# Row gathers made during the count fill: GpSimd waits for every second pair to land

## What is computed

```
feat = (h @ W).reshape(N, H, D)
e = leaky_relu(el[src] + er[dst], 0.2)
ex = exp(e - segment_max(e, dst)[dst])
alpha = ex / segment_sum(ex, dst)[dst]
rst = segment_sum(feat[src] * alpha[..., None], dst) + bias
...
h = z @ W
msg = h[row] * norm[:, None]
z = segment_sum(msg, col) + b
```

## Time and profile before

| | us |
|---|---|
| timed runs (3) | 5558.09, 5565.08, 5570.45 |
| median | 5565.08 |
| span of the profiled execution | 6940.0 |
| GpSimd busy / VectorE busy / TensorE busy | 2148.9 / 3284.3 / 4623.5 |
| mean granted TensorE clock | 0.815 |

### The profile page before, as it was taken

One profiled execution on the slowest core, in us unless ns is written; L12 is line 12 of the kernel. 1 busy time (PEld: TensorE's weight loads), 2 busy tenths in 40 slices (PEclk: granted clock), 3 DMA queues, 4 the chain that ended last, 5 costly groups with the idle time before them and its releaser, 6 DMA issues. The chain is left out here.

```text
span 6940.0 us, 113554 instructions
## 1 busy us (share of the span) xinstructions
PE 4623.5 (67%) x23328; PEld 3590.1 (52%) x23329; DVE 3284.3 (47%) x10456; ACT 2960.7 (43%) x7576; POOL 2148.9 (31%) x2057
## 2 busy tenths in 40 slices
PE   2411111366565677777777479799999998369997
PEld 1300000233323555555555479677777776369997
DVE  6511111487666666666666745533334333522222
ACT  0200000266666555555555523256655665623332
POOL 2477777300002555555555222100000000422221
PEclk8655555698767888888888589899999999589999
DMA  4377676322224656665566456547753444556665
GB/s 131 113 212 199 193 202 194 116 89 95 95 93 131 165 164 166 169 168 167 163 167 166 127 162 181 146 145 223 221 177 93 133 134 117 165 155 181 181 181 168
DMA packets 623736, 1084.57 MB, mean 156 GB/s; under 512 B 74390, under 2 KB 502093, under 8 KB 616748
## 3 DMA queue, kind: packets, MB, share of 16 engines
q1 hardware_dynamic: 504252, 733.75, 35.3%
q0 software_dynamic: 112144, 268.88, 15.3%
q10 hardware_dynamic: 7200, 80.28, 2.8%
HBM read 782.21 MB, written 309.57 MB: 157 GB/s over the span
## 5 line engine op out<-in xcount | busy, mean ns | idle before, releaser
L740 POOL DMA_INDIRECT arena<-table,arena x1664 | 1667.0, 1002 | 1909.3 <-DVE arena L877 1481.3
L686 PE MATMUL banks<-arena 128*128 128x392 bf16 x2368 | 654.0, 432 | 1198.9 <-issue 846.0
L1416 PE MATMUL banks<-parts,a_wide 128*128 128x512 f32 x4900 | 1179.9, 399 | 17.9 <-ACT a_wide L1439 17.9
L940 PE MATMUL banks<-arena 128*128 128x261 f32 x3328 | 1157.6, 487 | 0.0
L686 PEld LDWEIGHTS banks<-arena 128*128 128x128 bf16 x2368 | 342.1, 151 | 1510.6 <-issue 1470.8
L1416 PEld LDWEIGHTS banks<-parts,a_wide 128*128 128x128 f32 x4900 | 918.3, 189 | 262.9 <-ACT a_wide L1439 47.2
L1439 ACT CAST a_wide<-arena 128x896 fp32r<-128x896 f16 x700 | 658.9, 942 | 421.8 <-PE banks L1416 407.0
L709 ACT CAST arena<-banks 128x1568 f16<-128x1568 f32 x200 | 293.1, 1465 | 1261.2 <-issue 716.9
L940 PEld LDWEIGHTS banks<-arena 128*128 128x128 f32 x3328 | 701.9, 234 | 87.1
L2344 ACT ACTIVATE rings<-banks,b_sb 128x128 f32<-128x128 f32 x1296 | 370.6, 369 | 827.8 <-PE banks L2377 827.7
L658 DVE TENSOR_TENSOR arena<-arena 128x1024 bf16<-128x1024 f16 x296 | 203.9, 689 | 1083.2 <-issue 597.6
(11 more groups left out here) (367 smaller groups left out, 5313.2 us busy)
## 6 DMA issues: line engine op xcount, KB each, us to landing
arena<-counts SPq DMA_DIRECT2D x700, 224.0 KB, 2.5
arena<-in_L_ffn_W SPq DMA_DIRECT2D x114, 1024.0 KB
edge_rows<-arena SPq DMA_DIRECT2D x364, 264.0 KB
arena<-edge_rows SPq DMA_DIRECT2D x364, 264.0 KB
counts<-arena ACTq DMA_DIRECT2D x50, 1568.0 KB
arena<-in_L_ffn_w SPq DMA_DIRECT2D x64, 1024.0 KB
arena<-near_rows SPq DMA_DIRECT2D x416, 128.0 KB
expert_in<-rings SPq DMA_DIRECT2D x25, 2028.0 KB
```

Source lines behind the costliest of these rows:

```text
L686: last = pe.matmul(psum_all[:, bass.ds(bank, KEYS)], oh_b[:, p // LB % (OR // LB), :, p % LB], oh_k[:, p // KB % (OR // KB), :, p % KB], s ...
L740: pool.indirect_dma_start(out=got[:, r, j, :], out_offset=None, in_=table0, in_offset=bass.IndirectOffsetOnAxis(ap=src_sb[:, 2 * pair + j: ...
L940: last = pe.matmul(banks_a[u][:, 0:mw], onehot[:, u % GS, j, :], msg[:, u % RB, j, 0:mw], start=False, stop=False, skip_group_check=True)
L1416: last = pe.matmul(psum[u][:, 0:2 * D], a_wide[:, at:at + P], parts[:, a * 2 * D:(a + 1) * 2 * D], start=(a == 0), stop=(a == NT - 1))
```

## The change

In `fetch_edges`, after each kept pair with an odd number, GpSimd waits until that pair's two gathers have landed, before it issues the next.

```diff
@@ fetch_edges(pool) @@
                         for n in range(NKEPT):
                             turn, r = divmod(n, GS)
                             i, k = divmod(n, len(KEPT))
                             wait(pool, s_st[r], 16 * turn)
                             fetch(pool, r, pair_of(i, KEPT[k]), s_keep[r])
+                            if n % 2:
+                                pool.wait_ge(s_keep[r], 32 * (turn + 1))
```

## The result

The changed kernel takes 6134.50, 6156.90 and 6172.04 us, against 5561.59 us for the kernel before (median of four runs): a ratio of 1.1066, 95% interval 1.1044 to 1.1088. That is 593 us more. The direction was forecast, the size was not: 5885 us with a range to 6050. A fourth run, at 6682.56 us and a granted clock of 0.672, is in the median of all four (6164.47 us) and not in the ratio.

The account below looks back on a forecast made before the run. GpSimd's kept gathers were taken to bound the changed stage, with the fill hidden. Waits of 364 us, or 277 if gathers shorten, gave a middle of 320, added to the 5565 us median: 5885 us, range 5700 to 6050.

Parts of the forecast that it names:

- The gathers are the path, the fill is hidden, and the stall belongs to the profiled execution: Kept-pair stage: GpSimd's gathers last about 1004 us to 1279; the count fill beside them ends earlier, between 1104 and 1270.
- the stall: VectorE idle 19.80 us before each block of the count fill while gathers run; held to be largely the profiler's.
- the sum of idle times: Length less busiest engine outside 300 to 1291: 1268 us, too little for the 1375 us between span and timed runs.
- 182 waits of 2.3 us less 0.30, 364 us: GpSimd's added waits in the kept-pair stage: each costs issue end to landing, less the usual gap between gathers.
- Something may come back: Kept gathers: pauses may shorten those lengthened by crowded transfers, gaining 87 us, so the change costs 277 to 364.
- the rival of the late landings: Kept gathers land later beside the fill's 50 stores of counts: 195 us added, 6080 us; chance 0.12.
- A stall that the waits end: VectorE's fill idles in timed runs too; GpSimd's pauses free it, walk starts 523 us earlier: 5042 us; chance 0.11.
- a stall that stays: VectorE's fill idles in timed runs and still does, hiding some of the cost: 5600 to 5830 us; chance 0.13.

Follow-up runs that it names:

- again: The kernel before, profiled once more with no edit: 5562.08 us in one timed run.
- pair_before: Changed kernel with each of the 182 waits made to wait for the pair before the one just issued: 5673.63 us, 1.0224 of the kernel before.
- breath: Changed kernel with VectorE also waiting for its own last instruction behind each block of the count fill: 6006.32 us, 1.0797 of the kernel before.

## Why the prediction was wrong in size

1. *The gathers are the path, the fill is hidden, and the stall belongs to the profiled execution.* Right on the stall, and nearly so on the rest. The same program, profiled again, spans 5560.3 us, with no stall; the sum of idle times had pointed there. But in it the kept gathers end at 1278.8 and the fill's last block starts at 1283.7, so before the change both ended together, and the fill was the last by some 7 us. From its first block (278.1) the fill takes 1008 us, where I had 793 to 959: VectorE waits 248.3 us for TensorE there. The kept gathers take 1037 us, where I had 1004. Afterwards the gathers end 640 us behind the fill, so it hid next to nothing of the cost, as forecast.

2. *182 waits of 2.3 us less 0.30, 364 us.* This step was a third too small: the idle time of the kept gathers is 542.9 + 170.0 = 713 us against 225 in `again`, 488 us more. Three parts. GpSimd resumes later than SyncE, from whose stores I took the 2.3 us. The changed kernel has both behind one landing:

```profile
1508.41 0.95 POOL L740 DMA_INDIRECT arena<-table,arena  x1 [0.30 <-issue]
...
1511.72 0.37 SPq L765 DMA_DIRECT2D edge_rows<-arena  x1
...
1511.96 0.94 POOL L740 DMA_INDIRECT arena<-table,arena  x1 [2.61 <-DMA arena<-table,arena]
```

   The store starts 2.36 us behind the gather's end, as predicted, and the next gather 2.60. The 0.24 us between them is the same, within 0.01, at all 85 such places behind the fill: 0.24 x 182 = 44 us. Next, beside the fill a wait is 302.2 / 92 = 3.28 us, and 234.3 / 86 = 2.72 behind it: some 50 us. That is the rival of the late landings in its place, but at a quarter of its price; whether the stores of the counts cause it, as that rival had it, was not tried. The rest, some 30 us, is that behind the fill the stores start 2.43 us behind the gather on average, where I took 2.3 from three pairs. By the 2.0 us that the Trainium skill gives (DMA: Bandwidth & Descriptors, section "Anatomy of one DMA — SWDGE (gpsimd) path") the estimate was 309 us, further off. Its rule to issue early and wait late (same page, "Rules for kernel authors") is borne out by pair_before, 5674 us against 6157.

3. *"Something may come back", 0 to 87 us, of which I took 44.* The step that failed most, and by its sign. The kept gathers take 26.1 + 258.8 + 341.8 + 327.0 = 954 us in the changed kernel, and in `again` they took 30.6 + 255.8 + 530.4 = 817: 137 us more. Eleven gathers that stick account for some 190 us above the normal; the ones that now run behind the fill, at 945 instead of 1080 to 1163 ns, give some 50 back. I had a bound from 0 to a gain and no loss, on rows in which VectorE stood idle 19.8 of every 22.4 us: a trace with the fill stalled can't show what the fill does to a gather.

   488 + 137 = 625 us. From the end of the gathers to the walk's first score `again` needs 28 us, since its fill ends last, and the changed kernel 11: 625 - 17 = 608, and the two traces differ by 609 (the timed runs by 593). Against the 320 us of the forecast 124 are missing from step 2 (488 for 364) and 181 from this one (a loss of 137 for a gain of 44), less the 17 hidden: 288 of the 289 us.

4. *The rivals.* A stall that the waits end, and a stall that stays, are both excluded by `again`. The late landings came true in part, at a quarter of their price and with their cause not shown. The sticking gathers were not on the list.

## What to carry to other kernels

If the profiled span and the timed runs differ by a quarter, add up length less busiest engine by stage before you read any stall, and profile the same kernel again. A wait put behind asynchronous work costs the whole way to landing each time, and waiting one pair later costs a fifth of it here. And keep GpSimd's gathers back to back beside a dense VectorE: a gather issued some 2.4 us behind the one before cost up to 73 us here.

## What the runs showed of the hardware

- A gather issued 0.30 us behind another takes 0.95 to 1.30 us beside VectorE's back-to-back 16-bit compares (51 of 51 in one stretch of 74 us). One issued behind a wait can last until VectorE pauses: 73.41, 68.42, 19.19 us. Every one of over 4 us beside the fill, in all the traces, came 2.06 us or more behind the end of the gather before; what shorter gaps than that do is open. DMA was busy 0.07 in 296 to 370 then, against 0.67 in `again`.
- A pause of VectorE of 0.07 us let one through in the changed kernel, and with a pause of 0.04 us behind each block (breath) none stuck. A GpSimd memset is not held up (0.10 us).
- The Trainium skill (SBUF — State Buffer, section "SBUF: two separate sides") has VectorE and GpSimd share a pair of ports as an exclusive lock, which the one that starts first holds for its whole instruction. For a VectorE instruction with two SBUF inputs, as at L658 and L661, it says so only against a GpSimd instruction that reads SBUF; that GpSimd can't write a DMA's descriptors meanwhile it says of a two-port mode of VectorE. The unhindered memset, which reads nothing, agrees. The length does not: 73.41 us are 29 blocks of five instructions. The measurement decides. That it is this port that the gather lacks was not tried and stays open, as does why a gather close behind another is spared: behind a wait time has passed and the pair's own gathers have landed, and no run tells these two apart.
- One and the same program spanned 6940.0 us in one profiled execution and 5560.3 in another, with VectorE idle 19.80 us before each block in the first and not in the second. Why is open; no timed run of this kernel showed it (5553.91 to 5570.45 us).
